# The token MLP's pipeline runs on over the batches; row statistics and their columns are placed elsewhere

## The reference, cut to what matters

```
ln_out = layernorm(x, ln3_s, ln3_b)          # mean and variance over 512 features, eps 1e-5
mlp_out = gelu(ln_out @ w1 + b1) @ w2 + b2   # w1: 512 x 2048, w2: 2048 x 512
return x + mlp_out
gelu(x) = 0.5 * x * (1 + tanh(0.79788 * x * (1 + 0.044715 * x * x)))
```

## Time and profile before

| | us |
|---|---|
| median of 3 runs | 3742.41 (3740.49 to 3743.94) |
| the profiled execution, its own time | 3743.95 |
| its span | 3742.2 |
| mean granted TensorE clock | 0.967 |
| TensorE busy | 3455.5 (92%) |
| VectorE busy | 2347.7 (63%) |
| GpSimd busy | 2015.8 (54%) |
| ScalarE busy | 1833.4 (49%) |

### The profile page before, as it was taken

How to read it: one execution, slowest core, us unless ns; L and a number is a source line. 1 busy time by engine, 2 the same in 40 slices (tenths; PEclk the granted TensorE clock), 3 DMA queues, 4 the chain that set the end, 5 groups by cost and what they waited for, 6 DMA issues and landing times. The chain is left out here.

```text
span 3742.2 us, 59765 instructions
## 1 busy us (share of the span) xinstructions
PE 3455.5 (92%) x23516; PEld 2672.5 (71%) x23516; DVE 2347.7 (63%) x2908; ACT 1833.4 (49%) x4242; POOL 2015.8 (54%) x1079
## 2 busy tenths in 40 slices
PE   8989999999999999879999998799987888889878
PEld 6878778777877887568877776688875655656544
DVE  2455665566566556657778886545525677877776
ACT  2145664565466456557767765444532333333322
POOL 2234765575566556335556665445534566666653
PEclk9999999999999999989999999999998899999989
DMA  4231211121112111220021111200040000000000
GB/s 146 90 127 46 81 57 58 58 70 69 46 59 75 51 49 55 72 67 30 30 74 52 46 41 49 93 23 12 23 147 6 13 18 1 18 18 18 12 18 12
DMA packets 114303, 189.92 MB, mean 51 GB/s; under 512 B 17904, under 2 KB 36848, under 8 KB 113392
## 3 DMA queue, kind: packets, MB, share of 16 engines
q1 hardware_dynamic: 111856, 182.00, 14.4%
q10 hardware_dynamic: 2176, 4.19, 0.3%
HBM read 161.01 MB, written 25.17 MB: 50 GB/s over the span
## 5 line engine op out<-in xcount | busy, mean ns | idle before, releaser
L1025 POOL TENSOR_TENSOR l_pr<-l_pr,l_inv 128x1024 f32<-128x1024 f32 x256 | 480.0, 1895 | 382.8 <-DVE l_inv L1087 382.8
L895 ACT ACTIVATE l_pr<-l_ps_s,l_top 128x512 f32<-128x512 f32 x512 | 348.6, 690 | 352.4 <-DVE l_top L1083 271.6
L1529 POOL TENSOR_TENSOR tok_pr<-tok_pr,tok_ma 128x1024 f32<-128x1024 f32 x128 | 304.1, 2399 | 283.1 <-DVE tok_pr L1907 283.1
L2774 POOL TENSOR_TENSOR rec_rs<-rec_sE,rec_rT 128x1024 f32<-128x1024 f32 x128 | 326.8, 2555 | 215.7 <-DVE rec_sE L3262 166.7
L1020 POOL TENSOR_TENSOR l_x_lo<-ahead_piece,l_x_hi 128x1024 fp32r<-128x1024 f32 (+1 forms) x97 | 294.1, 3032 | 154.1 <-ACT l_x_hi L879 154.1
L1083 DVE TENSOR_REDUCE l_top<-l_ps_s 128x2 f32<-128x1024 f32 x256 | 304.1, 1218 | 10.5 <-PE l_ps_s L669 10.5
L3262 DVE TENSOR_TENSOR_SCAN rec_sE<-rec_wE,rec_ps_v 128x1024 f32<-128x1024 f32 x128 | 292.7, 2286 | 5.5 <-POOL rec_rs L2774 1.1
L679 PE MATMUL l_ps_t<-l_ident,l_pr 128*128 128x128 f32 x2048 | 275.2, 277 | 11.0 <-POOL l_pr L1025 4.9
L679 PEld LDWEIGHTS l_ps_t<-l_ident,l_pr 128*128 128x128 f32 x2048 | 225.6, 141 | 78.2 <-issue 60.7
L1779 ACT ACTIVATE tok_pr<-tok_pr,tok_shift 128x256 f32<-128x256 f32 x512 | 253.7, 498 | 13.4 <-DVE tok_shift L1915 12.0
L630 PE MATMUL l_ps_b<-l_x_hi,l_w_lo 128*128 128x256 f32 x784 | 226.8, 289 | 0.0
(11 more groups left out here) (507 smaller groups left out, 9833.5 us busy)
## 6 DMA issues: line engine op xcount, KB each, us to landing
ahead_piece<-x SPq DMA_DIRECT2D x63, 512.0 KB, 3.9
ahead_piece<-in_c SPq DMA_DIRECT2D x63, 512.0 KB, 4.8
ahead_rows<-x SPq DMA_DIRECT2D x22, 512.0 KB, 4.2
ahead_piece<-in_L_w_qk SPq DMA_DIRECT2D x16, 512.0 KB, 6.0
x<-tok_xb SPq DMA_DIRECT2D x16, 512.0 KB, 2.8
l_xt<-in_xT SPq DMA_DIRECT2D x8, 512.0 KB, 6.3
l_ct<-in_cT SPq DMA_DIRECT2D x8, 512.0 KB, 7.2
l_xn<-in_x SPq DMA_DIRECT2D x8, 512.0 KB, 4.8
```

The lines of the kernel that those rows point to most:

```text
L895: act.activation(pr[t][:, h, :], ps_s[:, t % 2, h, :], ACT.Exp, bias=top[:, t, h:h + 1], accum_out=mass[:, t, h:h + 1]).then_inc(exped, 1)
L1025: pool.tensor_tensor(pr[t][:, :, :], pr[t][:, :, :], inv[:, t, :].unsqueeze(2).to_broadcast([P, 2, FEAT]), ALU.mult).then_inc(scaled, 1)
L1529: pool.tensor_tensor(tile, tile, ma[u][:, :, :].rearrange("p t k -> p (t k)").unsqueeze(1).to_broadcast([P, 2, TT * TOK]), ALU.add).then_i ...
L2774: pool.tensor_tensor(rs[j % 2][:, :, :], sE[j % 2][:, :, :], rT[s][:, :, :], ALU.mult).then_inc(rs_made, 1)
```

## The change

1. TensorE, GpSimd, ScalarE and VectorE no longer close each batch with steps of its own. `order(drain)` runs n over 0 to 7 of all batches in turn, and `before(b, n, steps)` names the item some steps back, across the batches. So `outputs` 5, 6, 7 of a batch follow `hidden` 0, 1, 2 of the next, and the tanh, product, rounding and splitting of chunk 7 stand in step 0 of the next batch. Only after the last batch do they stand alone.
2. The addition of the rows and the store of batch b - 1 stand in step 3 (`Y_LAG`) of batch b, VectorE's addition ahead of that step's scaling, ScalarE's store at the step's end; `add_bias(b)` stands in step 4 (for batch 0 in step 7 as before).
3. `moment` moves to step 1, `normalise` to step 2, GpSimd's `power` to step 1. VectorE's copy and addition on `var_eps` go; GpSimd adds the epsilon from a constant tile ahead of the power. `moment` waits for `normalised` of the batch before.
4. The load of rows waits for `biased` only.
5. TensorE's idle turns ahead of the first hidden sums are 44 instead of 16.

```diff
--- before.py
+++ after.py
@@ -2052,7 +2052,7 @@
         w1_hi, w1_lo = (sb("w1_" + n, [P, FT, HID], F32R) for n in ("hi", "lo"))
         w2_hi, w2_lo = (sb("w2_" + n, [P, 2 * CHUNKS, FEAT], F32R) for n in ("hi", "lo"))
         ln_sb, b1_sb, b2_row = sb("ln_cols", [P, 2, FT]), sb("b1", [P, 2 * CHUNKS]), sb("b2", [P, FEAT])
-        ident, half_power = sb("ident", [P, P]), sb("half_power", [P, TT])
+        ident, half_power, eps = sb("ident", [P, P]), sb("half_power", [P, TT]), sb("eps", [P, TT])
         xs = [ahead.rows, sb("xs1", [P, TT, FEAT])]
         stats, moments, var_eps, rstd = sb("stats", [P, TT, 6]), sb("moments", [P, TT, 2]), sb("var_eps", [P, TT]), sb("rstd", [P, TT])
         xn = sb("xn", [P, TT, FEAT])
@@ -2075,7 +2075,7 @@
         half_loaded = [sem(f"half_loaded{i}") for i in range(3)]
         piece_hi, piece_split, half_hi, half_split = (sem(n) for n in ("piece_hi", "piece_split", "half_hi", "half_split"))
         loaded, stored = [here.rows_loaded, sem("loaded1")], sem("stored", 16)
-        counted, powered, normalised, biased = sem("counted", 4), sem("powered", 1), sem("normalised", 1), sem("biased", 1)
+        counted, powered, normalised, biased = sem("counted", 2), sem("powered", 2), sem("normalised", 1), sem("biased", 1)
         turned, turned_kept, ln_rounded, ln_split = sem("turned", 2), sem("turned_kept", 2), sem("ln_rounded", 2), sem("ln_split", 2)
         h_summed, squared, squared1, cubed, bent, gelled, hid_rounded, hid_split = (
             sem(n, CHUNKS) for n in ("h_summed", "squared", "squared1", "cubed", "bent", "gelled", "hid_rounded", "hid_split"))
@@ -2096,6 +2096,15 @@
                 return (w1_hi, w1_lo)[part][:, 2 * half:2 * half + 2, i * FEAT:(i + 1) * FEAT]
             return (w2_hi, w2_lo)[part][:, 4 * i + 2 * half:4 * i + 2 * half + 2, :]
 
+        def order(drain):
+
+            for g in range(BATCH * CHUNKS + drain):
+                yield g // CHUNKS, g % CHUNKS
+
+        def before(b, n, steps):
+            g = b * CHUNKS + n - steps
+            return g // CHUNKS, g % CHUNKS
+
         def halves_up_to(n, i):
 
             return HALVES.index((n, i, 1)) + 1
@@ -2109,7 +2118,6 @@
             open_loop(sp, loop_sems)
 
             def load(b):
-                sp.wait_ge(added, of(b - 2, 1, 0))
                 sp.wait_ge(biased, of(b - 2, 1, 0))
                 sp.dma_start(xs[b % 2][:, :, :], rows_of(x, b)).then_inc(loaded[b % 2], 16)
 
@@ -2142,7 +2150,8 @@
         def _(pool):
             make_identity(pool, ident, ident_made)
             pool.memset(half_power[:, :], -0.5).then_inc(const_made, 1)
-            pool.wait_ge(const_made, 1)
+            pool.memset(eps[:, :], 1e-5).then_inc(const_made, 1)
+            pool.wait_ge(const_made, 2)
 
             def split_hidden(b, k):
                 pool.wait_ge(hid_rounded, of(b, CHUNKS, k))
@@ -2150,8 +2159,10 @@
                                    ALU.subtract).then_inc(hid_split, 1)
 
             def power(b):
-                pool.wait_ge(counted, of(b, 4, 3))
+                pool.wait_ge(counted, of(b, 2, 1))
                 pool.wait_ge(normalised, of(b - 1, 1, 0))
+                pool.tensor_tensor(var_eps[:, :], moments[:, :, 1], eps[:, :], ALU.add).then_inc(powered, 1)
+                pool.wait_ge(powered, of(b, 2, 0))
                 pool.tensor_tensor(rstd[:, :], var_eps[:, :], half_power[:, :], ALU.pow).then_inc(powered, 1)
 
             def add_bias(b):
@@ -2161,20 +2172,19 @@
 
             power(0)
             pool.wait_ge(cols_loaded, 48)
-            for b in range(BATCH):
-                for n in range(CHUNKS + 1):
-                    if b == 0 and n == 7:
-                        pool.wait_ge(half_split, len(HALVES))
-                        add_bias(b)
-                    elif b and n == 1:
-                        add_bias(b)
-                    if n < CHUNKS:
-                        pool.wait_ge(squared1, of(b, CHUNKS, n))
-                        pool.tensor_tensor(cube[n % RING], cube[n % RING], pre[n % RING], ALU.mult).then_inc(cubed, 1)
-                    if n >= 1:
-                        split_hidden(b, n - 1)
-                    if n == 2 and b + 1 < BATCH:
-                        power(b + 1)
+            for b, n in order(1):
+                if b == 0 and n == 7:
+                    pool.wait_ge(half_split, len(HALVES))
+                    add_bias(b)
+                elif 0 < b < BATCH and n == Y_LAG + 1:
+                    add_bias(b)
+                if b < BATCH:
+                    pool.wait_ge(squared1, of(b, CHUNKS, n))
+                    pool.tensor_tensor(cube[n % RING], cube[n % RING], pre[n % RING], ALU.mult).then_inc(cubed, 1)
+                if b or n:
+                    split_hidden(*before(b, n, 1))
+                if n == 1 and b + 1 < BATCH:
+                    power(b + 1)
 
         @block.tensor
         def _(pe):
@@ -2222,16 +2232,16 @@
             keep_busy(pe, ps_h[0][:, 0, 0:P], ident, 14)
             turn(0, 0)
             turn(0, 1)
-            keep_busy(pe, ps_h[0][:, 0, 0:P], ident, 16)
-            for b in range(BATCH):
-                pe.wait_ge(ln_split, of(b, 2, 1))
-                for n in range(CHUNKS + Y_LAG):
-                    if n < CHUNKS:
-                        hidden(b, n)
-                    if n in TURN_STEPS and b + 1 < BATCH:
-                        turn(b + 1, TURN_STEPS.index(n))
-                    if n >= Y_LAG:
-                        outputs(b, n - Y_LAG)
+            keep_busy(pe, ps_h[0][:, 0, 0:P], ident, 44)
+            for b, n in order(Y_LAG):
+                if b < BATCH:
+                    if n == 0:
+                        pe.wait_ge(ln_split, of(b, 2, 1))
+                    hidden(b, n)
+                if n in TURN_STEPS and b + 1 < BATCH:
+                    turn(b + 1, TURN_STEPS.index(n))
+                if b or n >= Y_LAG:
+                    outputs(*before(b, n, Y_LAG))
 
         @block.scalar
         def _(act):
@@ -2276,21 +2286,25 @@
             act.wait_ge(cols_loaded, 48)
             keep_turned(0, 0)
             keep_turned(0, 1)
-            for b in range(BATCH):
-                for n in range(CHUNKS + 1):
-                    if n < CHUNKS:
-                        evict(b, n)
-                    if n >= 1:
-                        bend(b, n - 1)
-                    if b == 0 and n < len(HALVES) // 2:
-                        round_half(2 * n)
-                        round_half(2 * n + 1)
-                    if n >= 1:
-                        round_hidden(b, n - 1)
-                    if n in TURN_STEPS and b + 1 < BATCH:
-                        keep_turned(b + 1, TURN_STEPS.index(n))
+            def store(b):
                 act.wait_ge(added, of(b, 1, 0))
                 act.dma_start(rows_of(out, b), res).then_inc(stored, 16)
+
+            for b, n in order(1):
+                if b < BATCH:
+                    evict(b, n)
+                if b or n:
+                    bend(*before(b, n, 1))
+                if b == 0 and n < len(HALVES) // 2:
+                    round_half(2 * n)
+                    round_half(2 * n + 1)
+                if b or n:
+                    round_hidden(*before(b, n, 1))
+                if n in TURN_STEPS and b + 1 < BATCH:
+                    keep_turned(b + 1, TURN_STEPS.index(n))
+                if 0 < b < BATCH and n == Y_LAG:
+                    store(b - 1)
+            store(BATCH - 1)
             act.wait_ge(stored, 16 * (BATCH + 2))
 
         @block.vector
@@ -2302,17 +2316,14 @@
                 ins.then_inc(counted, 1)
 
             def moment(b):
-                dve.wait_ge(counted, of(b, 4, 0))
-
-                dve.tensor_copy(var_eps[:, :], stats[:, :, 2]).then_inc(counted, 1)
+                dve.wait_ge(counted, of(b, 2, 0))
+                dve.wait_ge(normalised, of(b - 1, 1, 0))
                 for m in range(TT):
                     ins = dve.bn_aggr(moments[:, m, :], stats[:, m, :])
                 ins.then_inc(counted, 1)
-                dve.wait_ge(counted, of(b, 4, 2))
-                dve.tensor_scalar(var_eps[:, :], moments[:, :, 1], 1e-5, None, ALU.add).then_inc(counted, 1)
 
             def normalise(b):
-                dve.wait_ge(powered, of(b, 1, 0))
+                dve.wait_ge(powered, of(b, 2, 1))
                 dve.wait_ge(turned, of(b - 1, 2, 1))
                 for m in range(TT):
                     ins = dve.tensor_scalar(xn[:, m, :], xs[b % 2][:, m, :], moments[:, m, 0:1], rstd[:, m:m + 1],
@@ -2343,33 +2354,38 @@
             split_turned(0, 0)
             split_turned(0, 1)
             split_piece(1)
-            for b in range(BATCH):
-                for n in range(CHUNKS + 1):
-                    if n < CHUNKS:
-                        dve.wait_ge(squared, of(b, CHUNKS, n))
-                        dve.tensor_scalar(cube[n % RING], cube[n % RING], 0.044715, 1.0, ALU.mult, ALU.add).then_inc(squared1, 1)
```

(42 more changed lines are left out.)

## The result

The changed kernel takes 3744.42 us (median of 22 runs, 3737.44 to 3753.11), the kernel before 3740.14 in the runs beside it (median of 22). The ratio is 1.0014, with a 95% interval of 1.0009 to 1.0020: slower by 3.4 to 7.5 us. The profiled execution took 3744.32 us.

The account below looks back on a forecast made before the run. TensorE was taken to bound the stage, busy 45.3 of 46.6 us in the last batch. First batch -1.0, last batch -1.0, six batches +2.4, clock +8.5: +8.9 us, 3751.3 us on the median; range 3736 to 3758.

Parts of the forecast that it names:

- Removed waits: TensorE's waits at outputs of chunk 0, the first turn and outputs of chunk 6 go: 3.4 us a batch.
- Wait A: At each batch boundary TensorE waits for VectorE's split columns of the next batch: 2.57 us, bounds 1.4 to 2.6.
- Wait B: Outputs of chunk 0 wait for VectorE's addition of the previous batch's rows in step 3: 1.3 us, batches 1 to 6.
- The clock: TensorE's clock falls after five of six boundary gaps, at 1.7 us each: +8.5 us.
- Rival 1: The boundary wait exists but costs no clock, none to two falls: 3742.8 us without any; chance 0.28.
- 44 turns: Before the first hidden sums, idle turns close TensorE's gap, so 18 matmuls run at full clock: -1.7 us.
- First batch: Hidden sums of batch 1 start 2.8 us ahead, then about 18 matmuls at half clock cost 1.8: -1.0 us.
- Last batch: It loses only its first wait, at outputs of chunk 0, and has no added wait there: -1.0 us.
- The order by itself: Batches 1 to 6, added waits less removed waits and one late restart: +0.4 us each, +2.4 in all.
- Rival 2: VectorE gets operands before GpSimd at step 7's product, so the boundary wait is 1.4 us: 3734.4 us; chance 0.15.
- Rival 3: The 44 idle turns run at 0.22 us, end 4.3 us too late and lose the clock gain: 3757 us; chance 0.03.

Follow-up runs that it names:

- experiment 1: The changed kernel, but in steps 5 and 7 VectorE splits the next batch's columns before waiting for that step's scaling; 3714.54 us, ratio 0.9935.
- experiment 2: As experiment 1, with the normalisation behind the addition of rows in step 3 instead of in step 2 (except batch 0); 3711.79 us, ratio 0.9925.
- Experiment 3: The changed kernel with 20 idle turns on TensorE before the wait for the columns at each batch boundary; 3737.96 us, ratio 0.9992.
- experiment 4: The kernel before with 44 idle turns instead of 16 and nothing else; 3735.97 us, ratio 0.9993.
- experiment 7: As experiment 2, with GpSimd's bias addition of batch 0 moved to step 1 of batch 1 and tile eps declared last; 3709.75 us, ratio 0.9921.

## Why the prediction was right, and where its sizes were off

The forecast was +8.9 us; the runs show +5.2 (from the ratio), the stage +5.6. Sign and mechanism held, and the time lies in the range.

- **Removed waits.** All three went, as computed.
- **Wait A.** Forecast 2.57, idle 2.4. Measured: from 2505.58, the start of the last matmul of outputs 4, to 2508.26 are 2.68; without a wait hidden sums start 0.23 after such a matmul, so they were 2.45 late, idle 2.28. The matmul after the first follows at 0.22 instead of 0.12, a late restart of 0.1. Together 2.55, and by so much the period shrank in experiment 1 (from 49.17 to 46.62), which shows that the wait came from VectorE's order.
- **Wait B.** The over-sized term: forecast 1.3 (0.9 to 1.7), measured 0.6 (from 2478.78 to 2479.52 are 0.74, less 0.12), idle 0.46 where the prediction named 0.8 to 1.6 as its sign. With its restart it is the 0.72 of experiment 2. Normalisation and addition ran undisturbed (0.99 and 1.21), each began 0.07 to 0.08 before the one ahead had ended, and TensorE started 0.05 after the addition, not 0.15. GpSimd's column instructions, 0.20 and 0.70 us, (the power at 2474.76) ended 0.8 before VectorE's product of step 2 began (2475.59), with which GpSimd's cube starts, so "either may come first" was wrong: they were sized by the row of 0.81 each. Six batches: 4 us of the forecast.
- **The clock.** Five falls of six were forecast and five came, at 1.5 us, not 1.7: 7.5 for 8.5. That it was five was luck: a choice between rows that disagreed. At 2.3 us of idle both happen here, and the 2.82 of experiments 1 and 2 cost no fall. Experiment 3 shows the cost apart from the wait. Rival 1, no more than two falls, is out by this count, not by the time: its 3742.8 us is nearer to the measured 3744.42 than the forecast's 3751.3. The Trainium skill ("TensorE: Matmul & The Clock Gate", "Why this matters for your kernels"), which asks for idle gaps under about 3 us, disagrees with the trace: five of six gaps of 2.3 us were followed by a fall.
- **44 turns.** Forecast -1.7; experiment 4 gives -1.8. The granted clock was 1.00 behind 44 transposes, and in experiment 3 behind twenty at each of the six boundaries after the first. The Trainium skill's remark ("TensorE: Matmul & The Clock Gate", Part 4: PE-mode transpose) that transposes do not count does not hold in this case.
- **First batch.** Forecast: hidden sums of batch 1 at 2408.85, 60.2 us after the first idle turn; measured 61.2. The fall of the clock after it cost 1.4 (the period behind it is 50.59, against 49.17), for 1.8. Together -0.4 for the forecast -1.0.
- **Last batch.** -0.8 for its first wait, where -1.0 was forecast.
- **Not foreseen.** The tile eps slowed each hidden matmul by 0.001 us, 1.5 us over the stage. It is inside the measured +5.6.
- **The order by itself**, without falls: forecast +2.4 over six periods (2.57 + 1.3 - 3.4 - 0.1 is 0.37 each, so 2.2). Measured 6 x (49.17 - 49.28) = -0.7, although 1.2 of slower pace is in it. From 2.2 to -0.7, wait B takes 4.1 us and wait A 0.7. The removed waits, with a restart each, were 3.6 us a batch (49.28 before, 45.69 in experiment 7 at the same pace) where the sum had 3.7, which gives 0.7 back, and the pace gives 1.2.

Sum of the measured terms: first batch -0.4, last batch -0.8, order -0.7, five falls +7.5: +5.6, the stage's. As a check, up to the first hidden sums of batch 1 the changed kernel took 61.2 us against 71.4, with three units (8.4) still owed: -1.8. The six periods from there to batch 7's took 302.5 against 295.7: +6.8. The rest took 55.96 against 46.83, of which 8.4 were owed: +0.7.

Rival 2 (VectorE before GpSimd at step 7's product, 3734.4 us) did not happen: 1.81 us for that product. Rival 3, overrunning turns, neither.

## What to carry to other kernels

When batches are joined into one pipeline, the covering work at the boundary goes with them: look for whatever was prepared in the last steps of a batch, and move its producer ahead of work that waits for the same step. Here a change that lost 5 us became a gain of 22.5 in the stage when two lines were moved. A short gap of the matmul engine can cost the gap and more than half as much again in clock (2.55 and 1.5 us here), so price both.

## What the runs showed of the hardware that I had not expected

- Moving tiles by 8 bytes (a 128x2 float32 tile declared ahead of them) changed the mean pace (start to start) of 128x256 matmuls from 0.1168 to 0.1178 us, in all six kernels with the tile there against the two runs without; moved behind the others, 0.1168 came back. Which of the moved tiles matters was not tried. The 128x512 outputs went from 0.2331 to 0.2334 and back.
- GpSimd's addition on 128x2 took 0.20 us and the power behind it 0.70; without the addition ahead of it, behind a split of 1.31 us, the power had taken 0.81.
- A VectorE subtraction that started 0.4 us after a GpSimd addition of 128x1024 took 2.71 us instead of 0.69. The Trainium skill ("SBUF — State Buffer", "SBUF: two separate sides") describes an exclusive lock of a port pair which the second of two such operations waits for in full. The trace agrees: the subtraction ended 0.55 after the addition did.
